# Moving finishing transposes, turns and projection halves behind the value products in a two-layer decoder kernel

## Chip, cores and metric

The kernel runs on one core of a Trainium2 chip. The metric is device time in microseconds for one execution of the whole program; the median of three runs of the kernel before is 846.44 us (845.86 to 849.4).

## The reference

Two decoder layers on x of shape 4 x 512 x 128, with a context of 4 x 77 x 128. Each layer adds to x, after a layer norm, self-attention, cross-attention and a feed-forward block:

```
x = x + L0_attn(layernorm(x))            # 16 heads of 8, rope, causal
x = x + L0_xattn(layernorm(x), ctx)      # 16 heads of 8, 77 keys
x = x + L0_ffn(layernorm(x))             # 8 experts, top 2 of them per token
x = x + L1_attn(layernorm(x))            # 16 heads of 8, no mask
x = x + L1_xattn(layernorm(x), ctx)      # one head of 128
x = x + L1_ffn(layernorm(x))             # quantized weights, conv over the sequence, silu
```

Both self-attentions are `softmax(q k^T / sqrt(8)) v` over 512 queries and 512 keys, then a projection with a bias.

## The kernel before

The program calls the layers A0 (self-attention), X0 (cross-attention), M0 (experts), A1 (self-attention), X1 (cross-attention), F1 (feed-forward). A unit is four heads of one batch row, so each attention has 16 units: 0 to 15 are A0, 16 to 31 X0, 32 to 47 A1. A unit of A0 or A1 has four chunks of 128 keys (`kt`, or c). Every engine has its order written out by hand: `unit_pe`, `unit_dve`, `unit_act`, `unit_pool` and `unit_sp` issue for unit g, chunk by chunk, and engines meet at semaphores only.

On TensorE a chunk consists of four scores (L684, keys x queries of one head, i = 0 to 3), and ahead of each of them some matmuls of the maxima (L574; A0 adds two mask matmuls, L578 and L579) of a later unit, since the softmax's shift of a unit is computed ahead. Behind score 3 stand the value products (`pv_pe`, L732, eight instructions) of the chunk before; in chunk 0 they are those of the last chunk of the unit before. Between these stand smaller blocks:

- the **finish** of the unit before (`finish_pe`, L751): four transposes of the unit's output, then on VectorE a reciprocal and a product (`finish_dve`, L760 and L764);
- the **turn** (`turn_pe`, L611): one transpose of the shifts of the next unit; VectorE copies it (L618) and SyncE puts it into the next unit's stack by DMA (`shift_sp`, L625), which the first score of that unit waits for;
- **tasks beside** (`beside_pe`), from a table `BESIDE` by unit and place. Place "a" belongs to chunk 0, "b" to chunk 1, "c" to chunk 3. A task is a transpose of normed rows (`turn`), a projection of them (`q`, `k`, `v`), the merging of four units (`merge`, L774), their output projection (`proj`, L793), or a piece of X1 (`cross_k`, `cross_v`, `cross_q`, `cross_score`, `cross_turn`, `cross_out`). `q`, `k`, `v` and `proj` come in two halves (part 0 and part 1); the others are issued whole as part 0.

Maxima, finishes, turns and tasks share four PSUM banks (three in A0 and X0); `take_bank` settles at build time which bank a block takes, and TensorE waits until the bank was emptied. Scores of A0 use two pairs of banks, a pair to each exponential (L709); scores of A1 use three single banks in turn, with one exponential each (L705). `scores_pe` waits for the exponential that reads the bank it is about to overwrite.

ScalarE runs in order (`unit_act`): the exponentials of a chunk in two pairs, j = 0 and j = 1; in chunk 0 the copy of the finished unit's output (`pv_out_act`, L744). It takes the result of a task at place "a" or "c" between j = 0 and j = 1 if `in_one` says so (every task but q, k and v), and behind j = 1 otherwise. GpSimd masks the exponentials of A0 (L717) before the value products read them. SyncE's DMAs are queued in order by `unit_sp`: the load of a later unit's stack (L638, L644), the shift, then loads of weights and of the experts' biases (b_gated, 2 MB).

Of the kernel before, what the change touches and what calls it, by code (L numbers as in the profile page):

```python
# [94 lines left out]
A0, X0, A1 = Attention("A0", 0, 0, S, True), Attention("X0", 1, 1, SC, False), Attention("A1", 3, 2, S, False)  # L95
# [156 lines left out]
def build(nc, d, out):  # L252
# [4 lines left out]
    with es:  # L257
# [350 lines left out]
        def turn_pe(e, g):  # L608
            e.wait_ge(s["neg"], g + 1)
            bank = take_bank(e, ("turn", g))  # L610
            e.transpose(bank[:].bitcast(BF16)[0:8 * QT, 0:P], neg[:, g % 2].rearrange("p j c h q -> p (j c h q)"),  # L611
                        identb[:]).then_inc(is_filled(("turn", g)), 1)
# [133 lines left out]
        def finish_pe(e, g):  # L746

            e.wait_ge(s["pv_out"], g + 1)
            bank = take_bank(e, ("finish", g), out=1)
            for j in range(QT):  # L750
                i = e.transpose(bank[:, j * P:(j + 1) * P], oT[:, g % 2, j * P:(j + 1) * P], ident[:])  # L751
            i.then_inc(is_filled(("finish", g)), 1)
# [250 lines left out]
        def unit_pe(e, g):  # L1003
            a, u = layer(g), finished_in(g)
            first = g == STREAMS[0].start or g == STREAMS[1].start
            short[0] = a is X0
            for c in range(a.kt):
                beside = maxima_beside(g, c)
                for i in range(4):
                    for k in beside[i]:  # L1010
                        max_pe(e, *k)
                    scores_pe(e, g, c, i)
                    if a is X0:
                        continue
                    if i == 0:
                        if c == 0:
                            beside_pe(e, g, "a", 0)
                        if c == 1 and a is not A1:
                            for t in turned_in(g):
                                turn_pe(e, t)  # L1020
                        if c == 2 and u is not None:
                            finish_pe(e, u)
                        if c == 3:
                            beside_pe(e, g, "c", 0)
                    if i == 3:
                        if c:
                            pv_pe(e, g, c - 1)
                        elif not first:
                            last_pv_pe(e, g - 1)
                    if i == 3:  # L1030
                        if c == 2 and a is A1:
                            for t in turned_in(g):
                                turn_pe(e, t)
                        if c == 0:
                            beside_pe(e, g, "a", 1)
                        if c == 1:
                            beside_pe(e, g, "b", 0)
                        if c == 3:
                            beside_pe(e, g, "c", 1)
                            if g == X0.first - 1:  # L1040
                                turn_pe(e, X0.first + 1)
            if a is X0:
                for part in range(2):
                    beside_pe(e, g, "a", part)
                last_pv_pe(e, g - 1)
                if u is not None:
                    finish_pe(e, u)
                if g + 2 <= last_of_stream(g):
                    turn_pe(e, g + 2)
                for part in range(2):  # L1050
                    beside_pe(e, g, "b", part)

        def unit_dve(e, g):
            a, u = layer(g), finished_in(g)
            for c in range(a.kt):
                beside = maxima_beside(g, c)
                for i in range(4):
                    for k in beside[i]:
                        max_dve(e, *k)
                    if a is A1 and c == 2 and i == 3:  # L1060
                        for t in turned_in(g):
                            turn_dve(e, t)
                    if a is not X0 and i == 0:
                        if c == 1 and a is not A1:
                            for t in turned_in(g):
                                turn_dve(e, t)
                        if c == 2 and u is not None:
                            finish_dve(e, u)
                if a is not X0 and c != 2:
                    beside_dve(e, g, "abbc"[c])  # L1070
                if c == 2 and a is A0 and g in NORM_IN:
                    after, b = NORM_IN[g]
                    normalise(e, after.ln, b)
                if c == 3 and g == X0.first - 1:
                    neg_of(e, X0.first + 1)
                    turn_dve(e, X0.first + 1)
                if c == 2 and g in INTEGERS_IN:
                    scales_dve(e, INTEGERS_IN[g])
# [21 lines left out]
        def turned_in(g):  # L1100

            return [g + 1] if g < last_of_stream(g) else []
# [1286 lines left out]
```

## Time and profile before

| what | before |
|---|---|
| median of the runs | 846.44 us |
| profiled execution: span from first to last instruction | 844.2 us |
| TensorE busy (matmul) | 689.9 us, 82% of the span |
| VectorE busy | 589.3 us, 70% |
| ScalarE busy | 414.1 us, 49% |
| GpSimd busy | 285.0 us, 34% |
| chain that ended last, by engine | PE 62%, DVE 18%, issue 7%, POOL 4%, DMA 4%, ACT 4% |
| costliest group of TensorE on that chain | value products, L732, 11% |

PE is TensorE, DVE VectorE, ACT ScalarE, POOL GpSimd, SPq SyncE's queue. Busy time is the union of an engine's instructions; ends of matmuls are modelled. A share over the whole span mixes stages with different limits, so the rows further down are read stage by stage and then instruction by instruction.

### The profile page before, as it was taken

The page shows a single profiled execution, that of the slowest core. Times are in us where ns is not written, and L with a number is a line of the kernel's source. Part 1 is how long each engine was busy: PE and PEld are TensorE (multiplying, and loading weights), DVE is VectorE, ACT ScalarE, POOL GpSimd, SP SyncE. Part 2 cuts the span into 40 slices and gives each one's busy share as a digit, 9 for nine tenths or more (in the row PEclk, how much of TensorE's full clock was granted, in tenths as well). Part 3 has the DMA queues.
Part 4 walks back from the last instruction along what each step waited for, and adds up shares of the span by engine and source line. Part 5 has one row for each costly group of instructions (what it writes and reads, how often), then busy time and mean ns, then how long its engine had stood idle before and what let it go on. Part 6 is the DMA issues. An engine that isn't in the chain of part 4 may idle for free.

```text
span 844.2 us, 14947 instructions
## 1 busy us (share of the span) xinstructions
PE 689.9 (82%) x4693; PEld 333.1 (39%) x4698; DVE 589.3 (70%) x1606; ACT 414.1 (49%) x708; POOL 285.0 (34%) x504
## 2 busy tenths in 40 slices
PE   2759999989888998239999973668899988999887
PEld 1334454444434445116666641212232322324443
DVE  3757678686646664738788753778889898962664
ACT  1332556555665443003333322137688787885454
POOL 4742454543532233723222320122423133230310
PEclk9875999998988657569999995559999999999998
DMA  7443665482232314311111113521122210000000
GB/s 217 150 176 107 190 183 155 125 262 78 83 93 53 94 47 128 96 36 38 43 41 45 39 29 105 169 75 52 63 90 89 64 52 26 26 2 1 0 26 26
DMA packets 74780, 71.27 MB, mean 84 GB/s; under 512 B 14560, under 2 KB 67168, under 8 KB 74704
## 3 DMA queue, kind: packets, MB, share of 16 engines
q1 hardware_dynamic: 72000, 64.84, 25.1%
q0 software_dynamic: 2272, 4.69, 1.8%
q8 instruction: 40, 0.66, 0.3%
q10 hardware_dynamic: 432, 0.79, 0.3%
q14 instruction: 36, 0.29, 0.1%
HBM read 41.90 MB, written 28.00 MB: 83 GB/s over the span
## 4 chain that ended last, share of the span: by engine, by line
PE 62%; DVE 18%; issue 7%; POOL 4%; DMA 4%; ACT 4%; SPq 1%; DVEq 0%; POOLq 0%; ACTq 0%
PE bank_pv L732 11%; DVE mx L590 9%; PE bank_turn L574 8%; PE bank_scores L2024 5%; PE bank_scores L684 4%; PE bank_scores L1774 4%; PE bank_turn L1759 4%; PE bank_scores L1759 4%; PE bank_turn L751 3%; POOL routed_tokens L1726 2%; PE bank_scores L1767 2%; PE bank_turn L793 2%; PE bank_turn L528 2%; DMA stk<-stack_A 1%; DVE stats L450 1%
## 5 line engine op out<-in xcount | busy, mean ns | idle before, releaser
L590 DVE TENSOR_REDUCE mx<-bank_turn 128x1 f32<-128x512 f32 (+3 forms) x452 | 260.6, 616 | 67.2 <-PE bank_turn L579 35.8
L574 PE MATMUL bank_turn<-stk 64*128 64x77 bf16 (+4 forms) x708 | 164.2, 314 | 29.4 <-DVE mx L590 17.7
L684 PE MATMUL bank_scores<-stk 64*128 64x512 bf16 (+4 forms) x576 | 176.4, 372 | 4.8 <-ACT probs L705 3.6
L709 ACT ACTIVATE probs<-bank_scores 128x1024 f32<-128x1024 f32 (+4 forms) x160 | 117.2, 768 | 111.7 <-PE bank_scores L684 111.4
L705 ACT ACTIVATE probs<-bank_scores 128x512 f32<-128x512 f32 x256 | 138.6, 605 | 35.3 <-PE bank_scores L684 34.3
L732 PE MATMUL bank_pv<-probs,vsl 128*32 128x512 f32 (+4 forms) x1152 | 143.0, 570 | 2.8 <-POOL probs L717 1.9
L574 PEld LDWEIGHTS bank_turn<-stk 64*128 64x128 bf16 x708 | 54.4, 102 | 134.5 <-DVE mx L590 63.2
L717 POOL TENSOR_SCALAR_AFFINE_SELECT probs<-probs 128x256 f32<-128x256 f32 x128 | 52.1, 410 | 78.1 <-ACT probs L709 76.8
L1742 POOL DMA_INDIRECT expert_outputs<-probs,y_at x39 | 37.4, 960 | 101.0 <-DVE probs L1661 98.0
L477 POOL TENSOR_TENSOR rstd<-var,mhalf 128x4 f32<-128x4 f32 x24 | 25.4, 1058 | 119.2 <-DVE var L456 119.1
L1806 ACT COPY okT<-bank_scores 128x512 f32<-128x512 f32 x39 | 22.9, 587 | 80.8 <-PE bank_scores L1767 80.8
L528 PE MATMUL bank_turn<-ident,xn 128*128 128x128 f32 x60 | 13.2, 358 | 57.0 <-DVE xn L471 57.0
L684 PEld LDWEIGHTS bank_scores<-stk 64*128 64x128 bf16 (+1 forms) x576 | 47.6, 97 | 30.0 <-ACT probs L705 18.0
L579 PE MATMUL bank_turn<-behind_even,even_q 64*128 64x128 bf16 x256 | 53.4, 230 | 0.0
L578 PE MATMUL bank_turn<-behind_pair,pair_q 64*128 64x128 bf16 x256 | 53.4, 230 | 0.0
L1774 PEld LDWEIGHTS bank_scores<-w,okT 128*128 128x128 f32 x312 | 37.7, 191 | 25.0 <-issue 25.0
L2024 PE MATMUL bank_scores<-f_w1c,w 128*128 128x512 f32 x96 | 46.0, 616 | 0.4 <-ACT w L537 0.4
L1774 PE MATMUL bank_scores<-w,okT 128*128 x312 | 43.9, 284 | 0.8 <-ACT okT L1806 0.8
L604 POOL CAST neg<-mx 128x16 bf16<-128x16 f32 x33 | 6.5, 198 | 111.5 <-DVE mx L590 98.1
L590 DVE TENSOR_REDUCE mx<-bank_scores 128x1 f32<-128x512 f32 x60 | 40.8, 680 | 3.0 <-PE bank_scores L574 2.9
L1759 PE MATMUL bank_turn<-w,probs 128*128 x80 | 42.5, 616 | 0.0
L542 ACT COPY xnT<-bank_turn 128x512 f32<-128x512 f32 x19 | 11.1, 584 | 56.9 <-PE bank_turn L528 56.9
(299 smaller groups left out, 1179.7 us busy)
## 6 DMA issues: line engine op xcount, KB each, us to landing
stk<-stack_A SPq DMA_DIRECT2D x64, 256.0 KB, 3.2
w<-in_M_w SPq DMA_DIRECT2D x12, 512.0 KB, 4.7
stack_A<-parts SPq DMA_DIRECT2D x15, 384.0 KB, 3.1
stack_A<-fill SPq DMA_DIRECT2D x8, 512.0 KB, 5.1
stk<-stack_X SPq DMA_DIRECT2D x16, 256.0 KB, 2.7
stack_A<-parts SPq DMA_DIRECT2D x15, 256.0 KB, 3.2
probs<-routed_tokens SPq DMA_DIRECT2D x39, 65.0 KB, 1.8
b_gated<-in_M_b SPq DMA_DIRECT2D x1, 2048.0 KB, 11.9
```

Of the source, the lines that this page charges most:

```text
L574: mm = e.matmul(o, stk[r, slot, 0, pp, qt * P:(qt + 1) * P], stk[r, slot, 1, pp, 0:keys], start=True, stop=not a.causal)
L578: e.matmul(o, half(pair_q, j), half(behind_pair, j), start=False, stop=False)
L579: mm = e.matmul(o, half(even_q, j), half(behind_even, j), start=False, stop=True)
L590: e.tensor_reduce(o.rearrange("p h q -> p q h"), bank_of((g, m))[:, 0:k * keys].rearrange("p (q h k) -> p q h k", q=len(tiles), h=len(hs)) ...
L684: mm = e.matmul(score_bank(g, kt, i)[0:a.kp, 0:S - q0], stk[r, slot, 1, pp, kt * P:kt * P + a.kp], stk[r, slot, 0, pp, q0:S], start=True, ...
L705: e.activation(probs[:, probs_of(g, kt), j + 2 * pp], score_bank(g, kt, i), ACT.Exp, scale=1 / math.sqrt(HD)).then_inc(s["probs"], 1)
L709: e.activation(probs[0:a.kp, probs_of(g, kt), j:HG:2, 0:n], bank_scores[0:a.kp, 2 * j:2 * j + 2, 0:n], ACT.Exp, scale=1 / math.sqrt(HD)).t ...
L717: e.affine_select(out=o, in_=o, compare_op=ALU.is_ge, fill=0.0, base=0, pattern=[[0, 2], [1, P]], channel_multiplier=-1).then_inc(s["maske ...
L732: mm = e.matmul(bank_pv[VW * h:VW * (h + 1), q0:S], vsl[0:a.kp, slot, kt, h, :], probs[0:a.kp, probs_of(g, kt), h, 0:S - q0], start=(kt == ...
L1759: e.matmul(hid[t % 2][z], x_inT[:, t % 2], w1[:, bass.ds(ex[t], 1), z * FF:(z + 1) * FF].rearrange("p o n -> p (o n)"), start=True, stop=T ...
L1774: mm = e.matmul(y_bank[:, 0:D], actT[:, c * P:(c + 1) * P], w2[:, bass.ds(ex[t], 1), c, :].rearrange("p o n -> p (o n)"), start=(c == 0), ...
L2024: e.matmul(bank, f_xT[:, b, j * P + tap:j * P + tap + P], f_w1c[:, tap], start=(tap == 0), stop=False)
```

## The change

In units of A0 and A1, TensorE issues finish, turn and both halves of a task behind the value products of their chunk; before, the finish, A0's turn and the first half stood behind the chunk's first score (i = 0). VectorE's `finish_dve` and `turn_dve` move to the end of the chunk's maxima in the same way, the finish ahead of the turn. A1's turn already stood behind the value products of chunk 2; it now follows the finish there. Units of X0, and the orders of ScalarE, GpSimd and SyncE, are as before.

```diff
                     scores_pe(e, g, c, i)
                     if a is X0:
                         continue
-                    if i == 0:
-                        if c == 0:
-                            beside_pe(e, g, "a", 0)
-                        if c == 1 and a is not A1:
-                            for t in turned_in(g):
-                                turn_pe(e, t)
-                        if c == 2 and u is not None:
-                            finish_pe(e, u)
-                        if c == 3:
-                            beside_pe(e, g, "c", 0)
                     if i == 3:
                         if c:
                             pv_pe(e, g, c - 1)
                         elif not first:
                             last_pv_pe(e, g - 1)
                     if i == 3:
-                        if c == 2 and a is A1:
+                        if c == 2 and u is not None:
+                            finish_pe(e, u)
+                        if c == (2 if a is A1 else 1):
                             for t in turned_in(g):
                                 turn_pe(e, t)
                         if c == 0:
-                            beside_pe(e, g, "a", 1)
+                            for part in range(2):
+                                beside_pe(e, g, "a", part)
                         if c == 1:
                             beside_pe(e, g, "b", 0)
                         if c == 3:
-                            beside_pe(e, g, "c", 1)
+                            for part in range(2):
+                                beside_pe(e, g, "c", part)
                             if g == X0.first - 1:
                                 turn_pe(e, X0.first + 1)
...
                     for k in beside[i]:
                         max_dve(e, *k)
-                    if a is A1 and c == 2 and i == 3:
-                        for t in turned_in(g):
-                            turn_dve(e, t)
-                    if a is not X0 and i == 0:
-                        if c == 1 and a is not A1:
+                    if a is not X0 and i == 3:
+                        if c == 2 and u is not None:
+                            finish_dve(e, u)
+                        if c == (2 if a is A1 else 1):
                             for t in turned_in(g):
                                 turn_dve(e, t)
-                        if c == 2 and u is not None:
-                            finish_dve(e, u)
```

## Rows read from the trace of the kernel before

**Rows 1.** Busy us (x instructions) of PE, PEld, DVE, ACT, POOL; PEclk; DMA share; GB/s.

```profile
77.50:241.70 164.20, 152.66 (x1603) 76.39 (x1604) 115.97 (x273) 96.87 (x154) 78.44 (x199) 0.96 0.46 143
563.00:766.00 203.00, 184.27 (x1224) 60.39 (x1221) 171.65 (x376) 158.58 (x303) 60.19 (x113) 0.98 0.15 48
```

**Rows 2.** Timeline (start, length, what, idle before), TensorE, unit 41, chunks 2 and 3.

```profile
686.15 0.39 PE L684 MATMUL bank_scores<-stk 64*128 64x512 bf16 x1
686.47 0.66 PE L751 MATMUL bank_turn<-ident,oT 128*128 128x128 f32 x4
687.06 0.60 PE L684 MATMUL bank_scores<-stk 64*128 64x512 bf16 x2
...
687.82 1.06 PE L732 MATMUL bank_pv<-probs,vsl 128*32 128x512 f32 x8
...
688.86 0.39 PE L684 MATMUL bank_scores<-stk 64*128 64x512 bf16 x1
...
690.03 0.39 PE L684 MATMUL bank_scores<-stk 64*128 64x512 bf16 x1
690.34 1.06 PE L732 MATMUL bank_pv<-probs,vsl 128*32 128x512 f32 x8
```

**Rows 3.** Timeline, ScalarE, unit 41, chunk 2: its first exponential.

```profile
686.66 0.60 ACT L705 ACTIVATE probs<-bank_scores 128x512 f32<-128x512 f32 x1 [0.42 <-PE bank_scores L684]
```

**Rows 4.** Timeline, TensorE, unit 41, chunk 0: the halves of a proj task.

```profile
679.09 0.39 PE L684 MATMUL bank_scores<-stk 64*128 64x512 bf16 x1
...
680.06 0.60 PE L684 MATMUL bank_scores<-stk 64*128 64x512 bf16 x2
...
682.02 1.06 PE L732 MATMUL bank_pv<-probs,vsl 128*32 128x512 f32 x8
683.02 0.71 PE L793 MATMUL bank_turn<-A_wo,okT 128*128 128x128 f32 x4
...
683.67 0.39 PE L684 MATMUL bank_scores<-stk 64*128 64x512 bf16 x1
...
683.89 0.38 PE L684 MATMUL bank_scores<-stk 64*128 64x512 bf16 x1
```

**Rows 5.** Timeline, ScalarE and TensorE, unit 4 (A0), chunks 0 and 1.

```profile
116.30 1.94 ACT L709 ACTIVATE probs<-bank_scores 128x1024 f32<-128x1024 f32 x2 [1.22 <-PE bank_scores L684]
...
117.64 0.23 PE L611 MATMUL bank_turn<-identb,neg 128*32 128x128 bf16 x1
...
118.29 0.33 PE L684 MATMUL bank_scores<-stk 64*128 64x384 bf16 x1
...
118.86 1.07 PE L732 MATMUL bank_pv<-probs,vsl 128*32 128x512 f32 x8
```

**Rows 6.** Timeline, ScalarE, TensorE and VectorE, unit 40, chunks 0 to 2.

```profile
668.30 0.57 ACT L1934 COPY w<-bank_turn 77x512 f32<-77x512 f32 x1
668.77 1.09 ACT L705 ACTIVATE probs<-bank_scores 128x512 f32<-128x512 f32 x2
...
672.19 1.16 PE L1942 MATMUL bank_scores<-x_v,w 77*128 77x128 f32 x8
...
673.77 0.69 DVE L590 TENSOR_REDUCE mx<-bank_turn 128x1 f32<-128x512 f32 x1 [1.15 <-PE bank_turn L574]
```

**Rows 7.** Timeline, TensorE, unit 2, chunk 1; then the stretch's busy times (columns above).

```profile
97.78 0.22 PE L611 MATMUL bank_turn<-identb,neg 128*32 128x128 bf16 x1 [1.57 <-ACT cos_sin L865]
...
99.38 1.93 PE L732 MATMUL bank_pv<-probs,vsl 128*32 128x512 f32 x8
...
98.40:101.70 3.30, 3.30 (x22) 1.13 (x19) 1.25 (x2) 1.58 (x2) 0.82 (x2) 0.50 0.53 166
```

**Rows 8.** Timeline, SyncE in unit 9 and TensorE at the start of unit 11.

```profile
170.85 0.53 SPq L625 DMA_DIRECT2D stk<-negT  x1
...
173.82 0.57 SPq L1173 DMA_DIRECT2D b_gated<-in_M_b  x1
...
188.52 0.23 PE L574 MATMUL bank_turn<-stk 64*128 64x128 bf16 x1 [2.74 <-DMA stk<-stack_A]
```

## Prediction

> **What bounds the kernel now.** I read the table of stages first [rows 1]. The change touches two of them: the 16 units of A0 (77.5 to 241.7 us) and the 16 units of A1 (563 to 766 us). In A0 TensorE is busy 152.7 of 164.2 us and VectorE 116.0; in A1 TensorE 184.3, VectorE 171.7 and ScalarE 158.6 of 203.0. So in A0 TensorE alone is full, and in A1 three engines are tied together. A busy share doesn't say which wait ends last, though, so I went on to the instructions in order of time, one chunk at a time. By "chunk" I mean the stretch from one first score to the next; its four scores are s0 to s3, their exponentials e0 to e3.
>
> *A1, the loop of a bare chunk.* A1 has three score banks, so s3 waits for e0 (L680). In one chunk s0 starts at 686.15 [rows 2] and e0 at 686.66, and it takes 0.60 [rows 3]: e0 is over 1.11 after s0. In the next chunk, which has nothing behind its first score, s0 is at 688.86 and s3 at 690.03, 1.17 later; the value products follow at 690.34 [rows 2]. The value products hold TensorE for 1.00 before something else starts (682.02 to 683.02) [rows 4]. A bare chunk is therefore 1.17 + 0.31 + 1.00 = 2.48 us, and what sets it is the time from s0 to the end of e0, in which TensorE has little to do. This is the point of my forecast: **the place behind the first score lies inside a wait that is there anyway.** The chunk with a finish in that place goes from s0 at 686.15 to the value products at 687.82, 1.67, against 1.48 in the bare chunk [rows 2]. The finish takes 0.59 from its start to the next score (686.47 to 687.06), and 0.19 of it shows.
>
> *A0, the loop of the first two chunks.* Here s2 of a chunk waits for the second exponential of the chunk before (L682). In unit 4 the two exponentials of chunk 0 run from 116.30 for 1.94, so to 118.24, and s2 of chunk 1 starts at 118.29; the turn had gone out at 117.64, in the time before that [rows 5]. The turn's place is covered too.
>
> **The change part by part.** No instruction is added or removed; only orders change, on TensorE and VectorE. ScalarE's, GpSimd's and SyncE's own orders stay, and that is where the moved blocks bite.
>
> *The switch saved.* A projection half behind s0: s0 at 679.09, next score at 680.06; two scores in a row stand 0.22 apart (683.67, 683.89), so the half costs 0.75. Behind the value products it costs 0.65 (683.02 to 683.67) [rows 4]. The new place is cheaper by 0.10 of TensorE's time.
>
> The Trainium skill (TensorEngine Tiling (Array Packing), Tiling Modes, Key Properties) says that a change of tiling mode drains TensorE. The trace agrees with 0.10 for one pair of switches [rows 4], and by that rule alone every moved block would be a gain; that is the first rival below.
>
> *Finishes in A1 (units 33 to 47, 15 times).* In the old place 0.19 shows; in the new one 0.59 shows whole. The turn, which followed the value products for 0.04 (687.82 to 688.86, 1.04 against 1.00) [rows 2, 4], now follows a finish of another shape. Its price there is not in the trace: between 0.04 and 0.24 (a switch like the one above plus its own stream); I take 0.16. Chunk 2 grows from 2.71 to 1.48 + 1.00 + 0.59 + 0.16 = 3.23, by 0.52, or 7.8 us over 15 units. VectorE covers part: it is busy 171.7 / 16 = 10.7 us a unit [rows 1], and TensorE's loop after the change is 3 x 2.48 + 3.23 = 10.7 as well, so where VectorE is behind, nothing is lost. Bounds 0 and 7.8; I take 0.3 each, **+4.5 us**.
>
> *Tasks that ScalarE reads in the middle of a chunk (A1, 14 places: three merges, five turns, three cross_q, two cross_turn, one cross_k).* `unit_act` (L1109) still takes the task's result between e1 and e2. Today the task is done by then: the copy of cross_turn starts at 668.30 and e2 follows at 668.77 with no idle time before either [rows 6]. After the change the task is issued behind the value products, 2.48 after s0 at the soonest, and is done about 0.66 later (a finish's length [rows 2]), at 3.1; e1 is over at about 1.6. So ScalarE stands still for some 1.5 us, with e2 and e3 queued behind the copy, and s1 and s2 of the next chunk wait for e2 and e3, because the three banks go round. With the copy's 0.5 and e2's 0.6, s1 of the next chunk starts 1.25 after s0, and e0 of that chunk, behind e2 and e3, ends 2.25 after it: s3 at 2.3 instead of 1.17, +1.1. The task itself, covered before but for 0.19, adds 0.4. Price of a place up to 1.5; where VectorE is the slower one, down to 0. What a long block behind the value products does to VectorE is to be seen today at cross_out (672.19, 1.16 long): VectorE then idles 1.15 before its next maximum [rows 6]. I take 0.7, nearer to the half than to the end because VectorE is busy 85% of this stage [rows 1]: 14 x 0.7 = **+9.8 us**.
>
> *Halves that ScalarE reads at the end of a chunk, and those for VectorE (A1: six of q, k and v, one cross_v and three proj).* The first half was mostly covered (+0.4), one bank comes free earlier and the switches go (-0.3): **0**, between -3 and +4 in all.
>
> *A0.* The finish in chunk 2 saves the switch, 15 x 0.10 = -1.5. The turn gains nothing, since s2 waits for the exponential anyway, and costs 0.04 behind the value products: 16 x 0.04 = +0.6. The halves that stood between s0 and s1 of chunk 0 (k in unit 2, v in unit 3, proj in 5, 9 and 13) delayed both exponentials, and with them s2 of the next chunk; I price each at 0.75 [rows 4], so 5 x 0.75 = -3.8. Three q in chunk 3 save a switch each and one load, -0.6. The three merges lose their cover on ScalarE as in A1, but the exponential behind them is short: 0. The turn of unit 2 waits 1.57 for a bank that ScalarE holds with k's result (L865), and the value products behind it take 1.93, at a granted clock of 0.50, against 1.07 [rows 5, 7]: when the turn stands a chunk later this wait has passed, 1.57 + 0.86 = -2.4. Against this, SyncE: its shift is queued behind the turn, and ahead of the 2 MB load of b_gated (170.85, then 173.82) and of unit 13's own load, for which TensorE stands still 2.74 until 188.52 [rows 8]. The shift goes out 0.7 to 2 us later in its unit, these transfers with it, while TensorE comes earlier: +1.4, between 0 and +3. Sum **-6.3 us**, between -11 and -2.
>
> X0 and the experts' stage are not touched; which bank each block takes shifts there, 0 +- 1.
>
> *Sum.* +4.5 + 9.8 + 0 - 6.3 = +8.0 on the span of 844.2: 852.2. The median of the runs shown is 846.4, 2.2 above the profiled span; on that footing **854 us**.
>
> **The rivals.**
> *1, faster: TensorE's own time decides.* If VectorE and ScalarE run so far behind that neither e0 nor e2 is what TensorE waits for, the switches are the whole effect: 30 finishes and 35 other blocks x 0.10 = -6.5, plus -6.2 from A0's halves and unit 2's wait: 846.4 - 12.7 = 834. For it: TensorE's 93% in A0. Against it: the bare chunk's s3 starts right behind e0 [rows 2, 3]. It decides if chunk 2 of A1 stays at 2.71 or below. The Trainium skill's rule on draining, above, is the mechanism of this one. Chance 0.15.
> *2, about the same: VectorE covers A1.* VectorE is busy 171.7 of 203 us [rows 1], and four banks can hold maxima for it; if that backlog outlasts the block behind the value products, ScalarE's standstill costs 0.3 a place instead of 0.7 and a finish 0.1: 4.2 + 1.5 - 6.3 = -0.6, so 844 to 849. Against it: VectorE's backlog ran out at cross_out [rows 6]. Chance 0.23.
> *3, slower still:* the standstills at their full 1.5, finishes at 0.52: 21 + 7.8 - 6.3 = +22.5, 869. It needs VectorE never to be behind. Chance 0.07.
>
> **How the numbers follow.** Forecast 0.55 (849 to 862, likeliest 854), rivals 0.15, 0.23, 0.07. The range takes in the bounds of A0 and of the finishes around the forecast, and leaves out most of rival 1 and rival 3: 839 to 865. About 0.5%, 4 us, is what a measurement of this kernel can tell from no change; with the forecast's lower edge inside that: faster 0.17, same 0.22, slower 0.61.
>
> **What would show it.** Right: in A1, chunk 2 of a unit is about 3.2 long, not 2.7; ScalarE has gaps of over 1 us ahead of the copies L1934, L782, L542 and L1879, ended by TensorE; A1 grows by 10 us or more while A0 shrinks by 4 to 9; the wait of 1.57 in unit 2 is gone, and the wait for unit 13's load is longer. Wrong: no such gaps on ScalarE, A1 not longer, or A0 not shorter. TensorE's clock stood at 0.50, its 1.2 GHz level, behind the wait in unit 2 [rows 7]; if it falls at other places in A0, that sum moves by 1 to 3 us either way.

## The result and the profile after

The changed kernel takes 882.78 us (878.63 to 884.43) beside 847.92 (845.86 to 852.31) for the kernel before on the same chip: 1.040 times as long, 95% interval 1.034 to 1.046. The direction was forecast, the size was not: +8 us said, +35 measured, and 882.8 lies above the range's end of 865. The profiled execution lasted 878.63, its span 876.5, so the traces compared here differ by 876.5 - 844.2 = 32.3 us. Behind the edits the changed kernel's lines carry numbers lower by 9 (L1934 is now L1925, L1879 is L1870); L574 to L765 are the same.

Where the time is: busy time of each engine in three stages, first of the kernel before, then of the one after (columns as in [rows 1]). Each stage runs here from first score to first score (A0's to that of X0, X0's to that of its last unit, A1's to that of its last chunk), so the lengths differ a little from those of [rows 1].

```profile
74.10:240.20 166.10, 154.72 (x1613) 78.08 (x1609) 117.41 (x274) 97.44 (x153) 78.29 (x199) 0.95 0.46 141
240.20:327.00 86.80, 78.33 (x559) 40.00 (x558) 52.42 (x224) 42.82 (x54) 23.94 (x40) 0.69 0.26 72
563.20:763.60 200.40, 181.71 (x1209) 59.60 (x1206) 170.80 (x374) 156.22 (x298) 60.19 (x113) 0.98 0.15 49
...
72.40:236.00 163.60, 148.83 (x1615) 78.83 (x1612) 116.03 (x274) 97.59 (x154) 77.77 (x200) 0.93 0.47 143
236.00:327.50 91.50, 85.33 (x561) 42.65 (x562) 52.97 (x224) 43.18 (x54) 23.43 (x37) 0.61 0.25 68
563.80:793.40 229.60, 206.02 (x1210) 64.66 (x1208) 170.69 (x372) 153.05 (x299) 59.92 (x113) 0.92 0.13 43
```

A0 is 2.5 us shorter, X0 4.7 longer, **A1 29.2 longer**; what is left of the 32.3 is 0.9. In A1 VectorE and ScalarE are busy for about as long as before (170.7 and 153.1 us, against 170.8 and 156.2) and have 29 us more for it. TensorE's busy time rose by 24, and its granted clock fell from 0.98 to 0.92: part of that is the same work at half the clock.

What TensorE waits for in A1, first before, then after (engine, line, waited for: us in total, times, longest):

```profile
PE bank_turn L574 <- DVE mx L590: 8.5, 16, 3.5
PE bank_scores L574 <- DVE mx L590: 3.8, 7, 1.0
PE bank_scores L684 <- ACT probs L705: 3.6, 8, 0.6
...
PE bank_scores L684 <- ACT probs L705: 13.8, 25, 0.9
PE bank_turn L574 <- DVE mx L590: 3.0, 9, 0.7
PE bank_turn L1841 <- DVE mx L590: 2.5, 1, 2.5
PE bank_scores L574 <- DVE mx L590: 0.8, 3, 0.4
```

Before, the longest sum was for VectorE's maxima, 8.5 + 3.8 = 12.3 us; after, these waits are 3.0 + 2.5 + 0.8 = 6.3, and the longest sum is for ScalarE's exponentials, 13.8 us in 25 waits. One of the places, unit 40, answers [rows 6]. TensorE in chunks 0 and 1 (start, length, what, idle before), then ScalarE, then VectorE:

```profile
675.01 0.39 PE L684 MATMUL bank_scores<-stk 64*128 64x512 bf16 x1
...
676.47 1.06 PE L732 MATMUL bank_pv<-probs,vsl 128*32 128x512 f32 x8
677.46 0.66 PE L1917 MATMUL bank_scores<-ident,w 128*77 128x128 f32 x4
...
678.06 0.39 PE L684 MATMUL bank_scores<-stk 64*128 64x512 bf16 x1
...
679.29 0.39 PE L684 MATMUL bank_scores<-stk 64*128 64x512 bf16 x1 [0.63 <-ACT probs L705]
...
680.74 0.39 PE L684 MATMUL bank_scores<-stk 64*128 64x512 bf16 x1 [0.58 <-ACT probs L705]
```

```profile
678.16 0.58 ACT L1925 COPY w<-bank_scores 77x512 f32<-77x512 f32 x1 [1.58 <-PE bank_scores L1917]
678.64 1.08 ACT L705 ACTIVATE probs<-bank_scores 128x512 f32<-128x512 f32 x2
```

```profile
683.64 1.89 DVE L590 TENSOR_REDUCE mx<-bank_turn 128x1 f32<-128x512 f32 x3 [2.42 <-PE bank_turn L574]
```

Read from the top: the task (L1917) goes out 2.45 us after s0 (675.01 to 677.46), behind the value products. ScalarE's in-order list has its copy between e1 and e2, so ScalarE stands still for 1.58 until 678.16, and e2 and e3 of the *same* chunk come behind the copy. By then TensorE is in the next chunk: its s1 (679.29) and s3 (680.74) wait for those late exponentials. Maxima stand in TensorE's list between these scores, so VectorE gets none either: its gap is 2.42, where [rows 6] had 1.15. ScalarE's gaps ahead of the other results are of the same kind. The group of the merges (count, busy time and mean ns of one, then idle time before them in all and what ended it), one turn of normed rows and one cross_q:

```profile
L782 ACT ACTIVATE okT<-bank_turn,A_bv 128x512 f32<-128x512 f32 x3 | 2.1, 687 | 4.7 <-PE bank_turn L774 4.7
...
659.49 0.59 ACT L542 COPY xnT<-bank_turn 128x512 f32<-128x512 f32 x1 [1.57 <-PE bank_turn L528]
...
664.09 0.69 ACT L1870 ACTIVATE w<-bank_turn,X_bq 128x512 f32<-128x512 f32 x1 [2.04 <-PE bank_turn L1863]
```

That is 4.7 / 3 = 1.6 us of standstill for a merge, 1.57 for this turn and 2.04 for this cross_q. Nine of the 14 gaps are 1.57 or 1.58 long; the longest, 4.88 ahead of cross_k's result, holds the 2.5 that the task itself waited for VectorE (L1841 above).

The chunk with a finish answers [rows 2]. TensorE, unit 41, chunk 2:

```profile
697.27 0.39 PE L684 MATMUL bank_scores<-stk 64*128 64x512 bf16 x1
...
698.75 1.07 PE L732 MATMUL bank_pv<-probs,vsl 128*32 128x512 f32 x8
699.75 0.66 PE L751 MATMUL bank_scores<-ident,oT 128*128 128x128 f32 x4
700.33 0.23 PE L611 MATMUL bank_turn<-identb,neg 128*32 128x128 bf16 x1
...
700.50 0.39 PE L684 MATMUL bank_scores<-stk 64*128 64x512 bf16 x1
```

It is 700.50 - 697.27 = 3.23 us long, where it was 2.71: 1.48 to the value products, 1.00 for them, 0.58 for the finish, 0.17 for the turn.

A0's two places of [rows 7, 8], TensorE in unit 2 and at the start of unit 11, and SyncE in unit 9:

```profile
95.33 1.07 PE L732 MATMUL bank_pv<-probs,vsl 128*32 128x512 f32 x8
...
165.31 0.53 SPq L625 DMA_DIRECT2D stk<-negT  x1
...
168.32 0.57 SPq L1164 DMA_DIRECT2D b_gated<-in_M_b  x1
...
183.06 0.28 PE L574 MATMUL bank_turn<-stk 64*128 64x128 bf16 x1 [4.93 <-DMA stk<-stack_A]
```

Unit 2's turn stands behind these value products, at 96.21, and waits for nothing; they take 1.07 again, not 1.93. Unit 11 stands still for 4.93 instead of 2.74.

### The profile page after: what moved, and what is told of

The parts are those of the page before. It is cut to its first block, busy times and chain, and to the rows that moved or that the text cites. A ratio compares the mean times of both kernels' runs of the same rounds, so it can differ in the third digit from the quotient of the medians.

```text
span 876.5 us, 14952 instructions
## 1 busy us (share of the span) xinstructions
PE 716.7 (82%) x4698; PEld 342.4 (39%) x4698; DVE 588.6 (67%) x1606; ACT 410.6 (47%) x708; POOL 283.4 (32%) x504
## 4 chain that ended last, share of the span: by engine, by line
PE 63%; DVE 14%; ACT 7%; issue 6%; DMA 4%; POOL 4%; SPq 1%; DVEq 0%; ACTq 0%; POOLq 0%
PE bank_pv L732 13%; PE bank_turn L574 6%; DVE mx L590 6%; PE bank_scores L684 5%; PE bank_scores L2015 5%; PE bank_scores L1765 4%; PE bank_turn L1750 4%; PE bank_scores L1750 4%; ACT probs L705 3%; PE bank_turn L751 3%; POOL routed_tokens L1717 2%; PE bank_scores L1758 2%; PE bank_turn L528 2%; PE bank_turn L793 2%; DMA stk<-stack_A 1%
## 5 line engine op out<-in xcount | busy, mean ns | idle before, releaser
L684 PE MATMUL bank_scores<-stk 64*128 64x512 bf16 (+4 forms) x576 | 182.4, 387 | 18.1 <-ACT probs L705 14.1
L574 PE MATMUL bank_turn<-stk 64*128 64x77 bf16 (+4 forms) x713 | 166.1, 320 | 25.7 <-DVE mx L590 13.1
L732 PE MATMUL bank_pv<-probs,vsl 128*32 128x512 f32 (+4 forms) x1152 | 150.7, 598 | 3.9 <-POOL probs L717 2.2
L705 ACT ACTIVATE probs<-bank_scores 128x512 f32<-128x512 f32 x256 | 133.3, 608 | 39.6 <-PE bank_scores L684 39.6
L574 PEld LDWEIGHTS bank_turn<-stk 64*128 64x128 bf16 x713 | 56.4, 105 | 104.3 <-DVE mx L590 44.6
L1797 ACT COPY okT<-bank_scores 128x512 f32<-128x512 f32 x39 | 22.8, 586 | 81.3 <-PE bank_scores L1758 81.3
L760 DVE RECIPROCAL rec<-bank_turn 128x16 f32<-128x16 f32 x43 | 11.0, 257 | 48.4 <-PE bank_turn L751 48.2
L590 DVE TENSOR_REDUCE mx<-bank_scores 128x1 f32<-128x512 f32 x55 | 37.3, 679 | 4.0 <-PE bank_scores L574 4.0
```

The lines of the kernel that those rows point to most:

```text
L574: mm = e.matmul(o, stk[r, slot, 0, pp, qt * P:(qt + 1) * P], stk[r, slot, 1, pp, 0:keys], start=True, stop=not a.causal)
L590: e.tensor_reduce(o.rearrange("p h q -> p q h"), bank_of((g, m))[:, 0:k * keys].rearrange("p (q h k) -> p q h k", q=len(tiles), h=len(hs)) ...
L684: mm = e.matmul(score_bank(g, kt, i)[0:a.kp, 0:S - q0], stk[r, slot, 1, pp, kt * P:kt * P + a.kp], stk[r, slot, 0, pp, q0:S], start=True, ...
L705: e.activation(probs[:, probs_of(g, kt), j + 2 * pp], score_bank(g, kt, i), ACT.Exp, scale=1 / math.sqrt(HD)).then_inc(s["probs"], 1)
L732: mm = e.matmul(bank_pv[VW * h:VW * (h + 1), q0:S], vsl[0:a.kp, slot, kt, h, :], probs[0:a.kp, probs_of(g, kt), h, 0:S - q0], start=(kt == ...
```

## The experiments

Most are built from one text, in which three functions say for each unit whether a block stands behind the value products ("late") or where it stood before:

```diff
                     if i == 0:
+                        if c == 0 and not late_task(g, "a"):
+                            beside_pe(e, g, "a", 0)
+                        if c == 1 and a is not A1 and not late_turn(g):
+                            for t in turned_in(g):
+                                turn_pe(e, t)
+                        if c == 2 and u is not None and not late_finish(g):
+                            finish_pe(e, u)
...
```

All three true is the changed kernel, all three false the kernel before. `finish_dve` and `turn_dve` move with their block. Ratios are to the kernel before on the same chip, with the 95% interval; in rows of e1 lines from L574 on are numbered 15 higher than in the kernel before (the others' rows shown are of kernels with its numbers, or name no line).

| kernel | us | ratio | A0 | X0 | A1 |
|---|---|---|---|---|---|
| before | 847.92 | 1 | 166.1 | 86.8 | 200.4 |
| after | 882.78 | 1.040 (1.034 to 1.046) | 163.6 | 91.5 | 229.6 |
| e1: after, ScalarE reads at the chunk's end | 854.89 | 1.006 (1.003 to 1.009) | 163.5 | 90.8 | 206.8 |
| e2: finishes alone late | 858.76 | 1.014 (1.007 to 1.020) | 168.6 | 90.4 | 207.7 |
| e3: tasks alone late | 869.81 | 1.028 (1.020 to 1.036) | 162.5 | 85.7 | 221.4 |
| e4: everything late in A0 alone | 847.45 | 1.000 (0.996 to 1.004) | 162.2 | 91.2 | 200.6 |
| e5: before, ScalarE reads at the chunk's end | 849.61 | 1.001 (0.996 to 1.006) | 167.8 | 89.6 | 204.3 |
| e6: the 14 coupled tasks of A1 alone late | 870.12 | 1.024 (1.014 to 1.034) | 166.1 | 92.4 | 221.1 |
| e7: A1's finish behind the third score | 847.92 | 0.999 (0.994 to 1.003) | 169.1 | 92.2 | 200.0 |
| e8: a choice of places | 844.19 | 0.994 (0.990 to 0.998) | 159.5 | 86.7 | 200.3 |
| e9: after, load of b_gated cut in 8 | 874.64 | 1.036 (1.030 to 1.042) | 156.7 | 91.4 | 229.6 |
| e10: e8, load cut in 8 | 839.44 | 0.992 (0.988 to 0.995) | 153.3 | 92.0 | 200.3 |
| e11: before, load cut in 8 | 845.36 | 1.000 (0.996 to 1.003) | 161.3 | 89.4 | 200.6 |
| e12: after, TensorE's gaps filled | 871.77 | 1.026 (1.019 to 1.034) | 162.3 | 92.1 | 224.4 |

Us are medians of the runs, stages are from the one profiled execution of each. A1 is 200.4 to 200.6 in the three kernels that leave all its orders as they were (before, e4, e11) and 229.6 in the two that have all of the change in it (after, e9), so lengths of A1 repeat well; those of X0 do not, as is said further down.

### Is it ScalarE's place in the chunk?

The changed kernel, but ScalarE takes every result behind the chunk's last exponential:

```diff
 def in_one(g, place):
-    return layer(g) is not X0 and BESIDE.get((g, place), ("q",))[0] not in ("q", "k", "v")
+    return False
```

> The change, with one more edit: ScalarE takes every task's result behind the chunk's last exponential instead of between the second and the third. Theory A (ScalarE's standstill): what made the change slow is that ScalarE waits in the middle of a chunk for a task that TensorE now issues at its end, 14 times in A1 at 1.1 to 1.5 us, and that TensorE's clock falls behind the pile of these waits in units 44 and 47 (some 9 us). Then this kernel takes 882.8 - 14 x 1.1 - 9 = 858, between 853 and 865, and the gaps of over 1.5 us ahead of ScalarE's copies are gone. Theory B (the long block behind the value products starves VectorE or simply adds its length): this edit changes little, 876 or more.

854.89 us, inside the 853 to 865 of theory A: 28 of the 35 us come back (in the traces' A1 22.8 of 29.2), and TensorE's order is that of the changed kernel. So most of the cost is the standstill, not the new places on TensorE. Unit 40 in this kernel, ScalarE:

```profile
669.85 2.07 ACT L720 ACTIVATE probs<-bank_scores 128x512 f32<-128x512 f32 x4 [0.54 <-PE bank_scores L699]
671.96 0.59 ACT L759 COPY oT<-bank_pv 128x512 f32<-128x512 f32 x1
672.52 0.58 ACT L1949 COPY w<-bank_scores 77x512 f32<-77x512 f32 x1
```

The four exponentials run in one piece, and cross_turn's copy (L1949) follows with no wait, since its task is done by then. A1 keeps 206.8 - 200.4 = 6.4 us of the loss, about what the finishes cost (below).

The control is the same edit in the kernel before:

> The kernel before, with ScalarE taking every task's result behind the chunk's last exponential. A control for the first experiment: if the 28 us that this edit gave back to the changed kernel came from ScalarE's standstill (theory A), it can give nothing of that kind here, where the tasks stand behind the first score and nothing stands still: 845 to 850. If taking results last is simply the better order for ScalarE (rival), this kernel gains as well: below 840.

849.61 beside 847.28, no difference within 0.6%. So the edit is no gain of its own that would merely have hidden the loss; it undoes what the change did. In its profile A1 is even 3.9 longer than in the kernel before; 2.4 of that is unit 34, 19.75 long at a granted clock of 0.74 where it was 17.33 at 0.90.

### Finishes and tasks apart

`late_finish` alone true:

> Only the finishes move behind the value products, in A0 and A1, on TensorE and VectorE; turns and tasks stay as in the kernel before. Theory A (the place behind the first score lies inside the wait for the first exponential): chunk 2 of A1 grows from 2.71 to 3.2, 15 times, +7.8 at most and some +5 after what VectorE covers; A0's saving of 1.5 goes against it: 848 + 4 = 852, between 849 and 856. Rival (saved switches of TensorE decide): 848 - 3 = 845.

858.76, ratio 1.014: more than expected. A1 grew by 7.3 us, 0.49 a unit, where 0.3 was forecast and 0.52 was its bound. A0 (168.6) and X0 (90.4) are longer too, but kernels that change nothing there reach the same lengths (e7), so only A1's share is read from this run.

`late_task` alone true:

> Only the tasks beside (whole ones and first halves) move behind the value products; finishes and turns stay as in the kernel before. Theory A: nearly all of the loss sits here, since only these are read by ScalarE in the middle of a chunk: 848 + 14 x 1.5 + up to 9 from the clock, less 5 in A0: 869 to 875. Theory B (any block behind the value products costs its length): 24 tasks of A1 x 0.4 = +10, 853 to 860.

869.81, as the theory had it; A1 grew by 21.0.

Only those 14 tasks late that ScalarE reads between e1 and e2 (three merges, five turns, three cross_q, two cross_turn, one cross_k):

```diff
+def late_task(g, place):
+    return layer(g) is A1 and in_one(g, place) and BESIDE.get((g, place), (None,))[0] in ("merge", "turn", "cross_q", "cross_turn", "cross_k")
```

> Only the 14 tasks of A1 that ScalarE reads in the middle of a chunk move behind the value products (three merges, five turns of normed rows, three cross_q, two cross_turn, one cross_k); all else as in the kernel before. Theory A: they carry the loss of A1: 848 + 14 x 1.5 = 869, between 863 and 874, the clock's fall in units 44 and 47 included or not. Rival (the other tasks and halves have a share in it): below 860.

870.12, and A1 at 221.1: the 14 coupled tasks are the whole loss of the tasks (20.7 of 21.0 us), and the halves and cross_v are worth 221.4 - 221.1 = 0.3, where 0 was forecast (the two kernels' clocks in unit 47 differ by more than that: its first three chunks are 15.46 long at 0.78 in e3, 16.13 at 0.71 in e6). 20.7 / 14 = 1.5 us a place, the upper price of the prediction, though not all of it is standstill, as e12 shows.

### Where the finish is mostly covered

The kernel before, with A1's finish behind the third score:

```diff
+                    if i == 2 and c == 2 and u is not None and a is A1:
+                        finish_pe(e, u)
```

> The finishes of A1 stand behind the third score (and VectorE's part behind the third group of maxima) instead of behind the first; all else as in the kernel before. Theory A (the finish is free as long as it stands ahead of the fourth score, which waits for the first exponential): chunk 2 of A1 stays at 2.7 us and the time at 846 to 851, though the finish is nearly as late as in the changed kernel. Rival (a late finish costs by being late, for VectorE or for its bank): chunk 2 of A1 at 3.0 or more, 852 to 858.

847.92, ratio 0.999. TensorE, unit 41, chunk 2:

```profile
692.63 0.39 PE L684 MATMUL bank_scores<-stk 64*128 64x512 bf16 x1
...
693.48 0.63 PE L751 MATMUL bank_scores<-ident,oT 128*128 128x128 f32 x4
694.04 0.39 PE L684 MATMUL bank_scores<-stk 64*128 64x512 bf16 x1
694.36 1.06 PE L732 MATMUL bank_pv<-probs,vsl 128*32 128x512 f32 x8
```

From s0 to the value products it is 694.36 - 692.63 = 1.73, about the 1.67 of [rows 2], and A1 is 200.0 long, as before. So it isn't the first score that matters: the cover is the wait for e0 ahead of the fourth score, and of a finish in either place ahead of it 0.19 to 0.25 us shows. Behind the value products nothing is waited for, and it shows whole.

### A0 alone

The three functions return `layer(g) is A0`:

> The whole change in the units of A0 only; A1's units as in the kernel before. Theory A: A0 gains some 5 by unit 9 (no wait in unit 2, earlier exponentials beside proj), gives 2 back at unit 13's load, and nothing is lost elsewhere: 843 to 847. Rival (A0's new order also slows X0 behind it, whose stage took 4.7 longer after the change): 848 to 851.

847.45, ratio 1.000. In the profile A0 is 3.9 shorter and X0, whose order is the same, 4.4 longer. The time lies between the theory's range and the rival's. That A0's new order is what slows X0 isn't shown: X0 is as long in e6 and e7, whose A0 has the order of before.

### A version that keeps what gained

A0's turns and tasks late; in A1 only five tasks of units 33 to 37, whose chunks had become shorter with the change; no finish late; ScalarE reads at the chunk's end:

```diff
+def late_task(g, place):
+    return layer(g) is A0 or (g, place) in ((33, "a"), (34, "a"), (34, "c"), (36, "a"), (37, "c"))
+def late_turn(g):
+    return layer(g) is A0
+def late_finish(g):
+    return False
```

> A pick by the chunk tables: in A0 the turns and tasks stand behind the value products; in A1 only five tasks do (units 33 a, 34 a and c, 36 a, 37 c); all finishes stay behind the first score, and ScalarE takes every task's result last. Theory A: A0 is shorter by some 4 to 8 (no wait in unit 2, later turns in the units where VectorE holds the banks), A1 by some 2 to 4, X0 as before: 836 to 842. Rival (A0's gain is eaten by the longer wait for unit 13's load and a lower clock in X0): 845 to 850.

844.19, ratio 0.994 (0.990 to 0.998): faster than before by a little, though short of the 842 hoped for. Its A0 is 159.5, 6.6 under that of before, and A1 is unchanged, so the 2 to 4 us expected there did not come. A0's places were the gain, as forecast, once the finish stays early.

### The wait for unit 13's load

b_gated's 2 MB go out in eight pieces, one after the other over later units, so that unit 13's stack isn't queued behind all of them:

```diff
-        later += [(b1_gated[:], halves[:, :, 1].to_broadcast([P, NE, FF]))]
+        later += [(b1_gated[:, i:i + 1], halves[:, i:i + 1, 1].to_broadcast([P, 1, FF])) for i in range(NE)]
```

> The kernel before with the same cut of b_gated's load, and nothing else. Theory: the wait of 2.74 us at the start of unit 11 goes, and with it part of the half-clock stretch behind it: 2.5 to 6 us below the kernel before, 841 to 845. Rival, the bytes only move to another unit's load: within 1.5 us of the kernel before.

> This is e8_pick with the 2 MB load of b_gated cut into eight pieces of 256 KB, one behind the other over later units, so that the load of unit 13's stack isn't queued behind 2 MB. Theory: the wait of TensorE at the start of unit 11 (2.74 us before the change, 4.93 with it) is a wait for bytes ahead of it in the DMA queues, so it goes to under 1 us, and the stretch at half clock behind it shrinks: 4 to 6 us below e8_pick, 838 to 841. Rival: the bytes only move, and a stack load of a later unit of A0 or X0 waits instead: 843 to 846, the time of e8_pick.

> The changed kernel with the same cut of b_gated's load. Theory: the wait of 4.93 us at the start of unit 11 goes, 874 to 879; A1 stays at 227 to 232 us. Rival, the bytes only move: 881 to 885.

In all three kernels the wait at the start of unit 11 is gone, and A0 is shorter by 4.8 (before to e11), 6.9 (after to e9) and 6.2 us (e8 to e10). The time follows that only in part. The kernel before gains nothing that can be measured (845.36 beside 846.53), as the rival had it. e10's 839.44 lies where the theory had it (838 to 841), but its ratio of 0.992 and e8's 0.994 have intervals that overlap, and so have e9's and the changed kernel's. In the profiles of e11 and e10 X0 gives back 2.6 and 5.3 (columns X0 of the table, against before and e8). The cause of the wait was right; that its removal shortens the program is not shown. e10 is the fastest of all that ran, 0.9% under the kernel before (interval 0.5% to 1.2%).

### The clock in A1

In the changed kernel TensorE's clock stands at 0.50 in parts of units 44 and 47; in the kernel before no such stretch lies there. Unit 44 does the same work as unit 40, 12.65 us each before; after, 15.06 and 19.80. Units 40, 43, 44 and 47 (47's first three chunks) of the changed kernel:

```profile
675.00:690.10 15.10, 13.22 (x87) 4.64 (x87) 11.64 (x25) 9.23 (x20) 1.93 (x4) 1.00 0.13 40
715.10:731.10 16.00, 13.91 (x85) 4.54 (x86) 12.12 (x23) 10.15 (x20) 3.16 (x10) 1.00 0.10 35
731.10:750.90 19.80, 17.85 (x88) 5.91 (x88) 11.69 (x25) 10.70 (x23) 1.92 (x4) 0.74 0.08 25
775.70:793.40 17.70, 15.21 (x54) 4.60 (x53) 0.95 (x2) 9.06 (x18) 2.54 (x7) 0.60 0.00 0
```

The test leaves the order and the waits of the changed kernel's own work, and puts matmuls that nobody reads into TensorE's gaps in units 44, 46 and 47: nine repeats of maxima, and fourteen into an idle bank (23 in all; the text on record says 25).

```diff
+        AGAIN = {(44, 0, 1): 3, (44, 1, 1): 3, (44, 1, 3): 3}
+        FILL = {(46, 2, 3): 2, (46, 3, 3): 2, (47, 0, 1): 4, (47, 1, 1): 4, (47, 1, 3): 2}
...
                     for k in beside[i]:
-                        max_pe(e, *k)
+                        max_pe(e, *k, AGAIN.get((g, c, i), 0))
+                    if (g, c, i) in FILL:
+                        fill_pe(e, g, FILL[(g, c, i)])
```

> The changed kernel, with 25 matmuls more whose results nobody uses, put where TensorE waits for ScalarE in units 44, 46 and 47: nine repeat a block of maxima ahead of the waiting second or fourth score, fourteen and two go into an idle bank, all of the size of a score and 0.22 us apart. The units' own work, waits and order are unchanged. Theory: of A1's 29 us some 9 are the granted clock's fall to 0.50 in units 44 and 47, which follows the stretch in which TensorE stands still for over a quarter of the time; with the gaps filled the clock holds: unit 44 goes from 19.8 to 15.5 to 16.8 us, the first three chunks of unit 47 from 17.6 to 12.3 to 14.5, A1 from 229.6 to 219 to 223, and the time from 882.8 to 872 to 877, though work was added. Rival: the units are long because of their waits, and the clock's level costs little of it: the units stay at 19 and 17 or longer, and the time is 883 to 888.

871.77, ratio 1.026 beside 1.040. The two intervals just touch (1.034), so the medians alone would not settle it; the units that were filled tell more. Units 43, 44 and 47 of it:

```profile
715.60:734.30 18.70, 16.84 (x84) 5.46 (x83) 12.39 (x23) 10.15 (x20) 3.19 (x10) 0.82 0.08 25
734.30:750.50 16.20, 15.52 (x97) 5.37 (x97) 11.40 (x24) 10.71 (x23) 1.93 (x4) 1.00 0.10 32
775.30:788.10 12.80, 11.51 (x62) 3.72 (x60) 0.95 (x2) 9.07 (x18) 2.55 (x7) 1.00 0.00 0
```

Units 44 and 47, filled, are at 1.00 and take 16.2 and 12.8 instead of 19.8 and 17.7: 3.6 + 4.9 = 8.5 us. The 16.2 holds the time of the repeats too: unit 40 took 15.1 unfilled, so up to 1.1 more may be the clock's. Unit 43, unfilled and the same in both kernels, fell to 0.82 in this execution and took 2.7 longer; A1's total (224.4) missed the expected 219 to 223 mainly for that reason. So the fall costs 3 to 5 us where it comes.

In the four kernels that leave these standstills unfilled (after, e9, e3, e6) the clock fell in units 44 and 47 each time and in unit 43 never. For unit 47 the filling is therefore the likely cause that it did not. For unit 44 a rival is left: the fall may only have come earlier, in unit 43. One execution of e12 was profiled, and no run tells the two apart.

The same reading takes the clock's share out of e6, whose units 44 and 47 are these:

```profile
730.90:749.00 18.10, 16.01 (x88) 5.74 (x87) 11.97 (x25) 10.83 (x23) 1.92 (x4) 0.81 0.08 27
772.50:788.60 16.10, 13.40 (x51) 4.33 (x50) 1.71 (x5) 9.18 (x18) 2.31 (x6) 0.71 0.00 0
```

e12's units hold a late finish each, which e6's do not: chunk 2 of unit 44 is 3.85 long in e12 and 3.15 in the kernel before, that of unit 47 3.04 and 2.45. So at full clock e6's units would be about 16.2 - 0.7 = 15.5 and 12.8 - 0.6 = 12.2 long, and its clock cost 2.6 + 3.9 = 6.5. What is left, 20.7 - 6.5 = 14.2 us, is 1.0 us a place. This is an estimate, but there is a stretch that needs none: units 36 to 43 are at 1.00 in all these kernels. They take 100.4 us before, 107.3 in e6 (seven of the 14 places and the task of an eighth, 1.0 a place), 103.2 in e2 (eight finishes, 0.35 each) and 110.1 after the change; 6.9 + 2.8 is the 9.7 that the change costs there.

## Why the prediction was right about the sign and wrong about the size

| term of the sum | forecast | measured | from |
|---|---|---|---|
| A1, finishes | +4.5 | +7.3 | e2 |
| A1, 14 coupled tasks | +9.8 | +14.2 at full clock, +6.5 by the clock | e6, e12 |
| A1, halves and cross_v | 0 | +0.3 | e3 - e6 |
| A0 | -6.3 | -2.5 (after), -3.9 (e4) | profiles |
| X0 | 0 | +4.7 | profile |

The parts of A1, 7.3 + 20.7 + 0.3 = 28.3, make up its 29.2.

**The coupled tasks: the mechanism was right, and the cover taken off its price was the mistake.** The working said that the task goes out 2.48 after s0, is done at 3.1, leaves ScalarE standing for 1.5, and that s1 of the next chunk then starts 1.25 after its s0. The trace of unit 40 has 2.45, 3.15 (675.01 to 678.16), 1.58 and 1.23 (678.06 to 679.29). (s3 came 2.68 after s0, 678.06 to 680.74, where 2.3 was forecast: ScalarE's copy of the unit before, L744, stands ahead of e0 as well.) From there the prediction took 0.7 of an upper price of 1.5 "because VectorE is busy 85% of this stage". That step failed: at full clock a place cost 1.0. VectorE's busy share says how much work it has, not that it can go on when TensorE stops: its maxima come from the same in-order list in which the scores now wait. When TensorE waits for ScalarE, VectorE's supply ends too, and its gap of 2.42 in unit 40 shows that its backlog ran out. [rows 6] had shown such a gap, and the prediction named it against rival 2 without drawing the price from it.

Some cover was there, and another number would have sized it better than the busy share: TensorE's own waits for VectorE's maxima, 12.3 us in A1 before and 6.3 after. Where such a wait stood, a standstill ahead of it cost little. In the kernel before, chunk 0 of unit 41 holds this one:

```profile
681.71 0.39 PE L574 MATMUL bank_scores<-stk 64*128 64x512 bf16 x1 [1.05 <-DVE mx L590]
```

In e6 the merge just ahead of that chunk made chunk 3 of unit 40 0.41 longer and this chunk 0.31 shorter, 0.1 in all. The price of 1.0 is a mean of such places and of dearer ones.

**The finishes: the same step again.** Chunk 2 was forecast at 3.23 and is 3.23 or 3.24 in nine of the 15 units. 0.52 a unit would be 7.8; 7.3 was measured. The cover by VectorE, which took it down to 4.5, was there only in places: in e2 units 39, 42 and 43, whose chunk 2 was 3.03 to 3.10 long already, lost nothing, while units 40 and 44 lost 1.1 each.

**The clock in A1 was not in the sum.** The prediction kept it for A0 only. Of A1's 29.2 us, 8.5 are the fall in units 44 and 47. At full clock the change would have cost some 21 in A1, against the 14.3 forecast. So the cover was taken some 6 us too large, and the clock, put at nothing, is the larger part of the miss in A1.

**Rival 3 came closest, in part by luck.** It had the standstills at 1.5 each, 21 us, and the finishes at their full price, 869, and was given 0.07. Its sum for A1, 28.8, is near what happened, but by its own mechanism a place is 1.0, and the clock, which it did not have, makes up the rest. What lies between 869 and 882.8 is elsewhere: A0 gained 2.5 and not 6.3 (3.8), X0 lost 4.7, and the median lies 6.3 above the profiled span, where 2.2 was allowed (4.1). Rivals 1 and 2 fall with chunk 2 at 3.23 and with ScalarE's gaps.

**A0, step by step.** Unit 2's wait went as forecast: chunk 1 of that unit is 2.67 long, where it was 5.38, -2.7 against -2.4 (in e3, whose turn stays early but whose k is late, it is 2.91, so k's new place is enough). A0 as a whole shrank by 2.5, less than the 4 to 9 named as a sign of being right. The load's wait grew by 4.93 - 2.74 = 2.2, forecast +1.4 between 0 and +3: the 2 MB of b_gated go out 8.9 after the start of their unit (168.32 - 159.4) where it was 7.5 (173.82 - 166.3), and the unit's wait comes earlier. The turn, put at +0.04 a unit, gained in some: chunk 1 of units 6 and 10 went from 2.93 to 2.50, of 8 and 12 from 2.88 to 2.64 (in e3, whose turns stay early, unit 8 keeps 2.88). The finish was put at -0.10 and costs +0.2, some +2 to +3 in all where -1.5 was put: in most units chunk 2 fell from 2.39 to 2.29, but chunk 3 rose from 1.57 to 1.87. The same 2.29 and 1.87 stand in e2, where finishes alone are late, and 2.39 and 1.57 in e3 and e8, where they are not. VectorE and TensorE in unit 5 of the changed kernel show how:

```profile
127.39 0.26 DVE L760 RECIPROCAL rec<-bank_turn 128x16 f32<-128x16 f32 x1 [0.30 <-PE bank_turn L751]
127.68 0.29 DVE L764 TENSOR_TENSOR otok<-bank_turn,rec 128x128 f32<-128x128 f32 x1
...
128.03 0.39 PE L574 MATMUL bank_turn<-stk 64*128 64x512 bf16 x1
```

VectorE waits for the late finish, empties its bank at 127.97, and 0.06 later the next maxima follow on TensorE; A0 has three banks. In units 1 to 13 of the changed kernel this distance is 0.06 every time, in the kernel before 0.74 in eleven of them, so TensorE now runs into that bank. The Trainium skill (TensorEngine Tiling (Array Packing), Tiling Modes, Key Properties) says that a change of tiling mode drains TensorE. The 0.10 by which chunk 2 shrank is as much as one pair of such switches in [rows 4], so the trace agrees; the bank takes back three times that in the next chunk. With the finish early and the rest late (e8) A0 is 159.5, -6.6; the prediction's terms without the finishes give -4.8, but that the sums are near each other is luck, since the terms are not. In e3, where tasks alone are late, the five halves of chunk 0, put at -0.75 each, gave 0.04 to 0.21: chunks 0 and 1 of unit 5 went from 3.16 and 2.86 to 3.08 and 2.86. Chunk 1 goes to 2.42 only where the turn is late too (e8), so it was not the halves alone that held it up. The merges in chunk 3, put at 0, gave 0.4 each (2.56 to 2.16 in units 4 and 8), and the q halves of units 7 and 11 gave 0.56 (3.19 to 2.63).

At the end of A0 unit 15 lost some 2 us: from its first score to that of X0 it is 12.3 long at a mean granted clock of 0.72, where it was 10.1 at 1.00.

**X0 stays open.** Its order is the same in all these kernels, and it lasted from 85.7 to 92.4 us. In e6 nothing ahead of A1 was changed, A0 took its 166.1, and yet X0 took this, beside 86.8 at 0.69 before and 91.5 at 0.61 after:

```profile
239.00:331.40 92.40, 88.08 (x559) 43.45 (x558) 53.16 (x224) 43.34 (x54) 23.70 (x39) 0.58 0.24 68
```

Over the kernels X0's length goes with its granted clock: 85.7 at 0.71 (e3), 86.7 at 0.69 (e8), 89.4 at 0.67 (e11), 92.0 at 0.62 (e10), 92.2 at 0.57 (e7). What sets the clock there was not tried, so the 4.7 us of X0 cannot be put down to the change, and neither can X0's return of A0's gain in e4, e10 and e11.

## What to carry to other kernels

Before a block is moved on one engine, look for where the engine that reads it has the read in its own list: if that place isn't moved as well, everything queued behind the read is late, and here that was 28 of 35 us, the clock's fall in it. A block costs little where its engine waits anyway (0.19 to 0.25 of 0.59 us anywhere ahead of the fourth score), and up to its whole length where it doesn't. Another engine's high busy share doesn't size the cover for a standstill if that engine is fed by the one that stands still; the waits for that engine, which the trace has, come nearer.

## What the runs showed of the hardware

With 23 matmuls more that nobody reads, two units were shorter by 8.5 us: TensorE's granted clock stood at 1.00 (its 2.4 GHz level) in them, where it had fallen to 0.50 (1.2 GHz) in all four kernels with the same standstills unfilled. Ahead of the fall in unit 44 TensorE had been busy like this, and behind it the clock is at half (columns as in [rows 1]):

```profile
731.00:734.40 3.40, 2.66 (x18) 0.57 (x16) 2.98 (x6) 2.56 (x5) 0.00 (x0) 1.00 0.41 140
734.40:737.80 3.40, 2.28 (x15) 0.75 (x11) 2.41 (x6) 2.49 (x6) 0.00 (x0) 1.00 0.00 0
737.80:741.20 3.40, 3.31 (x14) 1.38 (x15) 0.57 (x1) 1.49 (x4) 0.41 (x2) 0.54 0.00 0
```

At half clock the value products take 1.93 and cross_out 2.08 (738.25 and 740.12), against 1.07 and 1.16 in unit 40; and TensorE is busy 3.31 of 3.40 us there, so the work that a standstill held up is then also done at half speed. Units 39 and 43 have waits of the same kind and kept the full clock in this execution; why unit 43 lost it in e12's, and what decides where the clock falls, isn't known.
